# Attention value products: three 66-column matmuls per block in place of 130 + 65, the row sum from a ones column, four query tiles copied at once

## The reference

```python
q, k, v = (split_heads(layernorm(x) @ W) for W in (Wq, Wk, Wv))   # (8, 16, 1024, 64)
w = einsum('bhqd,bhkd->bhqk', q, k) / 64 + causal
w = softmax(w)
mask = clip((arange(s) + span_val * s) / 33, 0, 1)      # one value per head and key
w = w * mask
w = w / (sum(w) + 1e-8)
out = einsum('bhqk,bhkd->bhqd', w, v)
x = x + out @ Wo
```

## Time and profile before

| | value |
|---|---|
| median of 3 runs | 3856.89 us (3854.99 to 3860.36) |
| the profiled execution, its own time | 3857.66 us |
| its span, first to last instruction | 3855.9 us |
| mean granted PE clock, share of full speed | 0.98 |
| PE / PEld busy, share of the span | 91% / 82% |
| DVE / ACT / POOL busy | 78% / 61% / 21% |

### The profile page before, as it was taken

The page is one execution under the profiler, slowest core; times in us unless marked ns, Lnnn a source line. Parts: engine busy times, 40 slices in busy tenths (PEclk is TensorE's granted clock), DMA queues, the critical chain, the costliest instruction groups (busy, mean ns, idle before and its releaser), DMA issues. The chain is left out here.

```text
span 3855.9 us, 90130 instructions
## 1 busy us (share of the span) xinstructions
PE 3504.2 (91%) x29924; PEld 3151.9 (82%) x29924; DVE 3002.8 (78%) x4884; ACT 2365.9 (61%) x5622; POOL 820.8 (21%) x830
## 2 busy tenths in 40 slices
PE   0899996999999899989989998998999999599998
PEld 0899995888788788878878887887888888499998
DVE  7899984777777777777777777777777777599996
ACT  1454543676677667667767766776776777344544
POOL 2223221111122112112211211221121121123232
PEclk8999998999999999999999999999999999799999
DMA  6111114444534444444434444444444444211110
GB/s 211 63 55 52 54 36 129 102 102 105 130 96 118 103 116 111 108 119 99 121 97 116 114 110 114 98 119 100 116 114 102 110 109 109 92 40 51 57 49 34
DMA packets 162617, 374.13 MB, mean 97 GB/s; under 512 B 19696, under 2 KB 61552, under 8 KB 161776
## 3 DMA queue, kind: packets, MB, share of 16 engines
q1 hardware_dynamic: 162288, 370.30, 37.1%
HBM read 129.31 MB, written 39.58 MB: 44 GB/s over the span
## 5 line engine op out<-in xcount | busy, mean ns | idle before, releaser
L1233 ACT ACTIVATE at_eT_hi<-at_t_ps 128x512 f16<-128x512 f32 (+3 forms) x1536 | 745.3, 492 | 564.4 <-PE at_t_ps L1145 520.2
L1314 DVE SCALAR_TENSOR_TENSOR at_eT_lo<-at_t_ps,at_eT_hi 128x512 f16<-128x512 f32 (+3 forms) x1536 | 826.1, 551 | 163.0 <-ACT at_eT_hi L1233 132.6
L1225 ACT ACTIVATE at_e_rows<-at_s_ps,at_neg_max 128x1024 f32<-128x1024 f32 (+7 forms) x1024 | 767.0, 749 | 127.2 <-DVE at_neg_max L1308 126.3
L1145 PE MATMUL at_t_ps<-at_ident,at_e_rows 128*128 128x128 f32 x4608 | 778.8, 278 | 52.0 <-DVE at_eT_lo L1314 46.6
L1308 DVE TENSOR_REDUCE at_neg_max<-at_s_ps 128x1 f32<-128x1024 f32 (+7 forms) x1024 | 766.6, 749 | 41.8 <-PE at_s_ps L1135 30.4
L1131 PE MATMUL at_s_ps<-at_kh_st,at_q_st 128*128 128x512 f32 (+2 forms) x1536 | 581.1, 378 | 52.3 <-issue 25.4
L1159 PE MATMUL at_o_ps<-at_v_cols,at_eT_hi 128*128 128x130 f16 x4608 | 608.1, 221 | 19.0 <-ACT at_o_raw L1241 17.5
L1145 PEld LDWEIGHTS at_t_ps<-at_ident,at_e_rows 128*128 128x128 f32 x4608 | 503.6, 141 | 90.8 <-DVE at_eT_lo L1314 67.3
L1159 PE MATMUL at_o_ps<-at_v_cols,at_eT_lo 128*128 128x65 f16 x4608 | 566.8, 192 | 0.0
L1132 PE MATMUL at_s_ps<-at_kl_st,at_q_st 128*128 128x512 f32 (+2 forms) x1536 | 515.1, 343 | 0.0
L1159 PEld LDWEIGHTS at_o_ps<-at_v_cols,at_eT_hi 128*128 128x128 f16 x4608 | 434.0, 98 | 35.7 <-ACT at_o_raw L1241 21.7
(11 more groups left out here) (184 smaller groups left out, 7336.7 us busy)
## 6 DMA issues: line engine op xcount, KB each, us to landing
at_kh_st<-at_k_hi SPq DMA_DIRECT2D x256, 256.0 KB, 4.4
at_kl_st<-at_k_lo SPq DMA_DIRECT2D x256, 256.0 KB, 5.9
at_w_qk<-w_qk_split SPq DMA_DIRECT2D x65, 512.0 KB, 6.2
at_q_st<-at_q_hi SPq DMA_DIRECT2D x128, 256.0 KB, 3.9
at_q_st<-at_q_lo SPq DMA_DIRECT2D x128, 256.0 KB, 4.9
at_w_v<-w_v_split SPq DMA_DIRECT2D x66, 256.0 KB, 5.7
at_w_out<-w_out_split SPq DMA_DIRECT2D x64, 256.0 KB, 5.7
ffn_x_rows<-in_L_attn_query_dram SPq DMA_DIRECT2D x32, 256.0 KB, 2.8
```

The source lines that it names most:

```text
L1145: last = nc.tensor.transpose(t_ps[i % 2][:, b * P:(b + 1) * P], e_rows[:, n % 4, (k0 + b) * P:(k0 + b + 1) * P], ident[:])
L1225: nc.scalar.activation(e_rows[:, n % 4, :w], s_ps[n % 2][:, col:col + w], ACT.Exp, bias=neg_max[:, n % 4:n % 4 + 1], accum_out=e_sum[:, pa ...
L1233: nc.scalar.activation(eT[0][:, i % EBUF, :count * P], t_ps[i % 2][:, :count * P], ACT.Copy, scale=PSCALE).then_inc(sem("eT_hi"), 1)
L1314: nc.vector.scalar_tensor_tensor(out=eT[1][:, i % EBUF, :count * P], in0=t_ps[i % 2][:, :count * P], scalar=PSCALE, in1=eT[0][:, i % EBUF, ...
```

## The change

1. `v_cols` gets 132 columns a block and head: 64 high parts, the mask's high part, a column of ones (set once by POOL), then 64 low parts and the mask's low part (and again a column of ones, which nothing reads).
2. `value` issues three matmuls a block in place of two, all into the same 66 columns of PSUM: high e by the high 66 columns, high e by the low 65, low e by the high 66. The sum of the two halves and the sum of e are then made in PSUM.
3. `exp` has no `accum_out` any more, `e_sum` and `o_sum` and POOL's addition at L1024 are gone.
4. `o_ps` becomes two banks of four query tiles (4 x 66 columns), used in turn: four units of odd j, then four of even j. `copy_out` runs once in four units and copies 264 columns. Value matmuls wait for a copy once in four units, for the copy of two sets ago.
5. `ORDER` goes from (7, 0, 5, 1, 6, 3, 4, 2) to (7, 1, 5, 3, 6, 0, 4, 2). The bank for the second `o_ps` comes from `s_ps1`, which shrinks from two banks to one; the units at odd places have at most four blocks.
6. `o_raw` is double-buffered by pair; `normalise` waits for the four copies of the pair.

```diff
-VCOLS = 2 * (DH + 1)
-VPART = (VCOLS, DH + 1)
+VHI = DH + 2
+VCOLS = 2 * VHI
+PRODUCTS = ((0, 0, VHI), (0, VHI, DH + 1), (1, 0, VHI))
-ORDER = (7, 0, 5, 1, 6, 3, 4, 2)
+ORDER = (7, 1, 5, 3, 6, 0, 4, 2)
+OSET = 4
+NO = NU // OSET
-        s_ps = [pb(f"s_ps{i}", [P, 2 * CHUNK]) for i in range(2)]
+        s_ps = [pb("s_ps0", [P, 2 * CHUNK]), pb("s_ps1", [P, CHUNK])]
-        o_ps = pb("o_ps", [P, CHUNK])
+        o_ps = [pb(f"o_ps{i}", [P, CHUNK]) for i in range(2)]
@@ POOL
+            for vc in v_cols:
+                nc.gpsimd.memset(vc[:, :, :, DH + 1], 1.0).then_inc(sem("v_ones"), 1)
-            def outputs(g):
-                pool.wait_ge(sem("o_copied"), g * NU + (NU + AHEAD["o_copied"]))
-                nc.gpsimd.tensor_tensor(o_sum[:], o_raw[:, :, :DH + 1], o_raw[:, :, DH + 1:], ALU.add).then_inc(sem("o_sum"), 1)
+            def outputs(g, par):
                 pool.wait_ge(sem("rden"), g + 1)
@@ PE, value
-                if k0 == 0:
-                    pe.wait_ge(sem("o_copied"), g * NU + (n + AHEAD["o_copied"]))
+                if k0 == 0 and n % OSET == 0:
+                    pe.wait_ge(sem("o_copied"), g * NO + (n // OSET - 1 + AHEAD["o_copied"]))
+                o = o_ps[n // OSET % 2][:, j // 2 * VHI:(j // 2 + 1) * VHI]
                 for b in range(count):
-                    for s in range(2):
-                        last = nc.tensor.matmul(o_ps[:, :VPART[s]], eT[s][:, i % EBUF, b * P:(b + 1) * P], v_cols[par][:, k0 + b, a, :VPART[s]],
-                                                start=k0 + b == 0 and s == 0, stop=k0 + b == j and s == 1)
+                    for p, (s, at, w) in enumerate(PRODUCTS):
+                        last = nc.tensor.matmul(o[:, :w], eT[s][:, i % EBUF, b * P:(b + 1) * P], v_cols[par][:, k0 + b, a, at:at + w],
+                                                start=k0 + b == 0 and p == 0, stop=k0 + b == j and p == len(PRODUCTS) - 1)
@@ ACT
-                nc.scalar.activation(e_rows[:, n % 4, :w], s_ps[n % 2][:, col:col + w], ACT.Exp, bias=neg_max[:, n % 4:n % 4 + 1],
-                                     accum_out=e_sum[:, par, a * QT + j:a * QT + j + 1]).then_inc(sem("exp_done"), 1)
+                nc.scalar.activation(e_rows[:, n % 4, :w], s_ps[n % 2][:, col:col + w], ACT.Exp, bias=neg_max[:, n % 4:n % 4 + 1]).then_inc(sem("exp_done"), 1)
+                if n % OSET < OSET - 1:
+                    return
-                nc.scalar.activation(o_raw[:, a * QT + j, :], o_ps[:, :VCOLS], ACT.Copy).then_inc(sem("o_copied"), 1)
+                nc.scalar.activation(o_raw[:, par, a * QT + j % 2:(a + 1) * QT:2, :],
+                                     o_ps[n // OSET % 2][:, :OSET * VHI].rearrange("p (u d) -> p u d", d=VHI), ACT.Copy).then_inc(sem("o_copied"), 1)
@@ DVE, normalise
-                    dve.wait_ge(sem("o_sum"), g + (1 + AHEAD["o_sum"]))
-                    nc.vector.scalar_tensor_tensor(out=den[:], in0=e_sum[:, par, :], scalar=SUM_EPS * PSCALE, in1=o_sum[:, :, DH],
+                    dve.wait_ge(sem("o_copied"), g * NO + (NO + AHEAD["o_copied"]))
+                    nc.vector.scalar_tensor_tensor(out=den[:], in0=o_raw[:, par, :, DH + 1], scalar=SUM_EPS, in1=o_raw[:, par, :, DH],
```

More of the change, by code:

```diff
@@ L701 @@
 PIECES = ("x_turn", "q", "k", "v", "o_turn", "wo")
-AHEAD = {"exp_done": 2, "eT_lo": 2, "value_done": NG + 1, "o_copied": 1, "wo_added": 5, "v_cols": 2, "turned": NG,
-         "o_sum": 1}
+AHEAD = {"exp_done": 2, "eT_lo": 2, "value_done": NG + 1, "o_copied": 2, "wo_added": 5, "v_cols": 2, "turned": NG,
+         "o_norm": 2}
 def attention_weights(nc, ctx, args, dram, keep):
@@ L872, in attention @@
         e_rows = sb("e_rows", [P, 4, SEQ])
-        e_sum = sb("e_sum", [P, 2, NU])
         eT = [sb(f"eT_{part}", [P, EBUF, CHUNK], F16) for part in ("hi", "lo")]
-        o_raw = sb("o_raw", [P, NU, VCOLS])
-        o_sum = sb("o_sum", [P, NU, DH + 1])
+        o_raw = sb("o_raw", [P, 2, NU, VHI])
         den, rden = (sb(n, [P, NU]) for n in ("den", "rden"))
@@ L1009, in values @@
                 nc.gpsimd.tensor_copy(vc[:, :, :, DH], keep["mask_hi"][:, :, bass.ds(r * 2, 2)]).then_inc(sem("v_edge"), 1)
-                nc.gpsimd.tensor_copy(vc[:, :, :, 2 * DH + 1], keep["mask_lo"][:, :, bass.ds(r * 2, 2)]).then_inc(sem("v_edge"), 1)
+                nc.gpsimd.tensor_copy(vc[:, :, :, VHI + DH], keep["mask_lo"][:, :, bass.ds(r * 2, 2)]).then_inc(sem("v_edge"), 1)
                 for c in range(2):
@@ L1018, in values @@
                     pool.wait_ge(sem("v_hi"), 2 * g + (c + 1))
-                    nc.gpsimd.tensor_tensor(vc[:, rows, :, DH + 1:2 * DH + 1], vm, vc[:, rows, :, 0:DH], ALU.subtract).then_inc(sem("v_cols"), 1)
-            def outputs(g):
-                pool.wait_ge(sem("o_copied"), g * NU + (NU + AHEAD["o_copied"]))
-                nc.gpsimd.tensor_tensor(o_sum[:], o_raw[:, :, :DH + 1], o_raw[:, :, DH + 1:], ALU.add).then_inc(sem("o_sum"), 1)
+                    nc.gpsimd.tensor_tensor(vc[:, rows, :, VHI:VHI + DH], vm, vc[:, rows, :, 0:DH], ALU.subtract).then_inc(sem("v_cols"), 1)
+            def outputs(g, par):
                 pool.wait_ge(sem("rden"), g + 1)
-                nc.gpsimd.tensor_tensor(o_norm[:].rearrange("p j a d -> p a j d"), o_sum[:, :, :DH].rearrange("p (a j) d -> p a j d", a=2),
+                nc.gpsimd.tensor_tensor(o_norm[:].rearrange("p j a d -> p a j d"), o_raw[:, par, :, :DH].rearrange("p (a j) d -> p a j d", a=2),
                                         rden[:].rearrange("p (a j) -> p a j", a=2).unsqueeze(3).broadcast_to([P, 2, QT, DH]),
@@ L1039, in pair @@
                 if before:
-                    outputs(g - 1)
+                    outputs(g - 1, 1 - par)
                 if after:
@@ L1044, in pair @@
                     root(b + 2)
-            pool.sem_inc(sem("o_sum"), AHEAD["o_sum"])
-            over_pairs(pool, start, pair, lambda: outputs(BATCH * PAIRS - 1))
+            pool.sem_inc(sem("o_norm"), AHEAD["o_norm"])
+            over_pairs(pool, start, pair, lambda: outputs(BATCH * PAIRS - 1, 1))
         @block.tensor
@@ L1096, in piece @@
                     if c == 0:
-                        pe.wait_ge(sem("o_norm"), gp + 1)
+                        pe.wait_ge(sem("o_norm"), gp + (1 + AHEAD["o_norm"]))
                     for i in range(GROUP):
@@ L1233, in turn_hi, with copy_out @@
                 nc.scalar.activation(eT[0][:, i % EBUF, :count * P], t_ps[i % 2][:, :count * P], ACT.Copy, scale=PSCALE).then_inc(sem("eT_hi"), 1)
-            def copy_out(n, g):
+            def copy_out(n, g, par):
+                if n % OSET < OSET - 1:
+                    return
                 a, j = UNITS[n]
                 act.wait_ge(sem("value_done"), g * NG + (LAST_GROUP[n] + 1 + AHEAD["value_done"]))
-                if n == 0:
-                    act.wait_ge(sem("o_sum"), g + AHEAD["o_sum"])
-                nc.scalar.activation(o_raw[:, a * QT + j, :], o_ps[:, :VCOLS], ACT.Copy).then_inc(sem("o_copied"), 1)
+                if n == OSET - 1:
+                    act.wait_ge(sem("o_norm"), g - 1 + AHEAD["o_norm"])
+                nc.scalar.activation(o_raw[:, par, a * QT + j % 2:(a + 1) * QT:2, :],
+                                     o_ps[n // OSET % 2][:, :OSET * VHI].rearrange("p (u d) -> p u d", d=VHI), ACT.Copy).then_inc(sem("o_copied"), 1)
             def start():
@@ L1256, in pair @@
                     elif kind == "copy":
-                        copy_out(i, g + dg)
+                        copy_out(i, g + dg, par ^ (dg & 1))
                     elif kind == "x_turn_hi":
```

2 lines of the change are left out of this document (1 added, 1 removed).

## The result

The changed kernel takes 3928.48 us (median of 4 runs, 3927.58 to 3931.43) against 3856.82 us before: a ratio of 1.0188, 95% interval 1.0174 to 1.0202. It is 72 us slower, where 67 us less was forecast; the time lies outside the range.

The account below looks back on a forecast made before the run. PE was taken to pace the attention, with 187 us of waits recoverable. Terms +12 - 25 - 18 - 36 = -67 us against 3857.7 gave 3791, set at 3790 us; range 3715 to 3865.

Parts of the forecast that it names:

- +12 us: PE's value products: three matmuls a block in place of two cost 2.5 ns more over 4608 blocks, 12 us.
- the third weight load: PE's value products: the added load a block was taken to fit under a 65-column matmul, costing nothing beyond the 12 us.
- case C: Rival, PE's value products: weight loads at 44 ns, block 132 ns, 3981 us; chance 0.10 with any other slower way.
- The copy's wait, -25: PE's value matmuls: their 48 waits for ACT's copy go, 25 us with drain; other bound 0.
- The exponential and the parts of e, -18 and -36: PE's waits: exponential done earlier, 18 us less; high and low parts of e done earlier, 36 us less.
- The pass-through of 19%: ACT to PE through DVE: 0.19 of ACT's freed 184 us reaches PE, 35, rounded to 36 us.
- The new order, zero: Query tile order in the attention: units 0, 1 and 3 change places at no cost, 0 us.
- case D: Rival: new order adds a DVE-maximum stall per pair head, 77 us, 3867 us; chance 0.07 with a balance within 0.2%.
- POOL and DVE, zero: Side engines: POOL's addition goes off the path, denominator work keeps its size, no DMA is added or moved; 0 us.

Follow-up runs that it names:

- b_split: Kernel before with its 130-column value matmul cut into two of 65 columns, three matmuls a block: 3969.15 us, ratio 1.0294.
- b_split_open: Kernel before with the 130-column value matmul cut into two and the inner loop written out on PE: 3881.17 us, ratio 1.0063.
- b_open: Kernel before with the inner loop written out on PE alone, as a control: 3863.57 us, ratio 1.0019.
- a_sum: Changed kernel with PE's inner loop written out, old tile order and the accumulator read back in every exponential (sum unused): 3839.46 us, ratio 0.9954.
- a_open: Changed kernel with the inner loop written out on PE alone, all other engines and work the same: 3839.73 us, ratio 0.9958.
- best: Changed kernel with all PE attention loops written out and the old tile order, rows picked by place when transposed: 3807.27 us, ratio 0.9875.

## Why the prediction was wrong

**The step that failed** is the one on the three matmuls, "+12 us", with its sentence that the open point was the third weight load. I costed 4608 more matmuls by their columns and loads, as work that streams past, and not as code inside a loop; the growth of the code stood in the sum at nothing. The body of PE's inner loop grew from 1600 to 1863 recorded instructions, and 16 jumps back went from free to 5.5 us each: 88.7 us in the changed kernel, 88.0 us in `b_split`, both by writing the loop out. A jump is a standstill of 3.5 us on average, 3.7 with the drain, and then a low clock: what the granted clock lacks of full speed adds up to 1.5 to 3.1 us over the 12 us behind each inner jump, 2.2 on average. That makes 5.9 us, an estimate from the trace, and covers the 5.5 without anything for ACT and DVE filling up again.

The trace of before held the warning in two places. PE waited 25.4 us for "issue" in 6 waits, 9.8 us at the start of the attention and 2.9 to 3.3 us at each of the five outer jumps; and ACT waited 37.2 us, 16 times, at its own inner jump. The prediction left the first out of its sum and does not mention the second. The Trainium skill (Runtime: NRT & Kernel Launch, section Instruction fetch mechanics) says as much: code is prefetched in sequence, in blocks of 256 instructions, and a taken branch whose target is not in the window must wait for a fetch. The traces agree in kind, but not in extent. The window there is of two such blocks, and here a body of 1600 recorded instructions jumps back without a wait. Nor is the limit at the 2048 instructions that the section gives for PE: 1863 recorded ones already stall (instructions that the profile does not record would come on top). Where it lies between the two no run shows.

**Three matmuls a block.** Right in kind, small in size: case C is out, a block takes 92.5 ns and not 132 or 243. But it costs 5 ns more than before and not 2.5; measured by `b_split_open` against `b_open` it is 17.6 us for the forecast 12. The missing nanoseconds stand behind the matmul that reads the low halves.

**The copy's wait, -25.** 15 us by the second bank alone, inside the bounds of 0 and 25; of the 10 that are missing, some 4 are in longer other waits, drain and all, and the rest is less than the scatter of that run.

**The exponential and the parts of e, -18 and -36.** This is the second wrong step. The pass-through of 19% treated ACT's freed time as one pool. With a copy after each unit the read's 92 us bring nothing with one bank (1.0009), where the wait for the copy grows by 15.5 us, and some 5 us with two; with one copy in four the same read is worth 19 us. So the failed term is the share passed on: it is no fixed share of ACT's freed time, and a second saving on ACT sets what the first is worth. The change as a whole, apart from its code and its order, does better than these singles: from `b_split_open` (3881.2) to `a_sum` (3839.5) 41.7 us. If the second bank is worth 15 there too, some 26 are left for three copies in four left out and what goes with them (POOL's addition, ACT's shorter code), which no run took apart; then 19.1 for the read.

**The new order, zero.** It costs 19.3 us, most of it in waits of the scores for the exponential, not for DVE as case D argued. Case D had the sign and a price of 77, with a chance of 0.07 that the whole would come out even.

The balance against the kernel before: written-out code +7.8, third matmul +17.6, bank and copies -41.7, read -19.1, order +19.3: -16.1, and `a_open` is 16.0 faster. Then +88.7 for the jump gives +72.7; measured 71.7. The five terms are differences along one chain of kernels, so that they close by construction; the jump was measured twice, and the two agree more closely than the five extra stalls of `b_split` give reason to expect.

**POOL and DVE, zero:** nothing in the traces speaks against it, though the addition was not tried alone. But the sentence there that no DMA is added holds for the data alone: the queue of PE's code took 162 packets more (301 against 139).

## What to carry to other kernels

Before an edit that puts more instructions into a loop, count the engine's instructions between two jumps and look for waits for "issue" at the first instruction of a body; near the limit a few hundred instructions can cost more than all their work, and to write the loop out for that one engine takes it back. Look at the bytes of the instruction queue in the page before and after: here they doubled when the loop stopped staying. Code that is written out raises them too (4.37 MB in `a_open`), without a stall, so that the waits have to be read beside them. And time freed on an engine off the path has no price of its own: here the same read was worth nothing, 5 or 19 us, depending on what else that engine still had to do.

## What the runs showed of the hardware

A standstill of PE of some 3.3 us at a jump is mostly followed by a stretch at a low granted clock: 0.50 to 0.68 over 4.5 us behind each of the 21 jumps in the changed kernel, and 0.61 over 4.4 us behind the outer jump at 1988.6 in the kernel before. Not always: behind the outer jump at 1653.0 there, after a standstill of 3.2 us, it stayed at full speed.

```profile
1988.60:1993.00 4.40, 4.27 (x22) 3.69 (x23) 2.21 (x3) 0.60 (x1) 0.00 (x0) 0.61 0.03 7
...
1653.00:1657.50 4.50, 4.32 (x33) 3.63 (x33) 2.72 (x4) 1.75 (x4) 0.00 (x0) 1.00 0.03 7
```

Three f16 weight loads in a row hide under three matmuls of 65 or 66 columns, 30.8 ns each on average. Code of PE that is written out is fetched while it runs without a visible stall: `best` moves 4.11 MB through the instruction queue and has one wait of PE for "issue", 9.7 us, at the start of the attention.
